# Four attention layers on one core: nine hand-written tables of steps put in another order

## The chip, the cores and the metric

The kernel runs on one core of one Trainium2 chip. The metric is the device time of one execution in microseconds (us); less is better. Three timed executions and one profiled execution of the kernel before are given.

## What is computed

64 batches of 64 tokens with 256 features (`x`) pass through four cross-attention layers against the same context (`ctx_2048`, 64 batches of 64 keys with 256 features). In layer 0 the "sequence" is the 256 features and the 64 tokens are the channels. The mask is all true in the inputs, but the kernel reads it. Cut to what matters:

```python
# layer 0: channels are the 64 tokens, attention runs over the 256 features
Mn = conv1x1(Wn, bn, inorm(x));  Mm = conv1x1(Wm, bm, inorm(ctx))
A  = softmax(einsum('bct,bcs->bts', Mn, Mm));  Ml = conv1x1(Wl, bl, ctx)
x  = conv1x1(Wo, bo, einsum('bcs,bts->bct', Ml, A)) + x
# layers 1 and 2: 16 heads of 16 features
a  = layer_norm(ctx) * ln_gamma + ln_beta
Q, K, V = heads(x @ Wq.T), heads(a @ Wk.T), heads(a @ Wv.T)
x  = x + tanh(gate) * (softmax(Q K^T / 4, mask) V) @ Wo.T
# layer 3: one head of 256 features, no norm
x  = x + alpha * (softmax((x w_q^T)(ctx w_k^T)^T / 16) (ctx w_v^T)) w_o^T
```

## The kernel before

**Groups and software pipeline.** The 64 batches are worked in eight groups of eight (512 tokens). A group first goes through a front part (its x and context are turned, normalised and projected, and layer 0 is computed) and then through layers 1, 2 and 3. The program runs these staggered: iteration g of the loop computes layers 1 to 3 of group g and, in between, the front part and layer 0 of group g+1. A start-up (prologue) loads and prepares all weights and does the front part of group 0, and a last iteration (tail) has no next group.

**Engines.** TensorE (PE) does every product and every transpose. Wide products are exact sums of three: each operand is split into a high and a low part, and `split_product` (lines 389 to 391) multiplies high by high, high by low and low by high. ScalarE (ACT) makes the high parts, the exponentials, and most copies out of PSUM. VectorE (DVE) makes the low parts, the row maxima and the subtractions of them, the normalisations by the sums, and the residuals. GpSimd (POOL) normalises the next group and builds its mask matrix. SyncE (SP) issues the DMAs.

**What sets the order.** No scheduler does. Nine strings list the steps of an engine, one after the other: `PE_ORDER`, `ACT_ORDER`, `DVE_ORDER` for an iteration, `..._FIRST` for the start-up and `..._TAIL` for the last iteration. Each engine runs its own list in that order and waits, at each step, on semaphores. The PE list also hands out the eight PSUM banks: the n-th fill of a table goes to bank n modulo 8 (`fills_of`, line 113), so a step of PE waits until the occupant eight fills before it has been read out (`wait_banks`). A moved step therefore changes which release its successors wait for.

**Names of the steps** (layer number behind the letter, then a part):
- `xT`, `cT`, `nT`: x, context and normalised context turned (lines 454 and 469 on PE); `Mn`, `Mm`, `V0`: projections of layer 0 (526, 481).
- `S`: scores (646 for layer 0, 659 for layers 1 and 2, 670 for layer 3) and on DVE the maxima and subtraction (1029; 1033 and 1037; 1042 and 1045). `X`: the exponential on ACT (855, 860, 863); `X3` on DVE: sums of layer 3 (1051, 1053). `T`: the weights turned (679, 703), copied out by ACT (874, 876, 878). `A`: weightings, that is the product with the values (726 for layer 0, 733 for layers 1 and 2), and on DVE the division by the sums (1064 to 1070 for layer 0, 1076 and 1078 else).
- `Q`, `K`, `V`, `O`: query, key, value and output projections (389 to 391); `AT`: the result of a layer turned; `XN`, `PV`: the last turn and the last product of layer 3 (679, 558), with DVE line 1021.
- `H.n` on ACT and `L.n` on DVE: high and low part of one half of the state (841, 968). `Q1.0` and `Q1.1` need `L.0` and `L.1`, `Q2.0` and `Q2.1` need `L.2` and `L.3`. There is one buffer for a half, so `H.1` comes after `Q1.0`.
- `ST`, `MV`: statistics of the next group (1087, 1095). `SC`: the mask column of the group (847).
- Start-up only: `Wq1` and so on: a weight turned (620), its high part on ACT and its low part on DVE (1140); `MT`, `MS`: mask turned and summed (572, 587); `GT`: a few vectors turned (577), copied out by DVE (1115); `WB`: DVE builds the block matrices of layer 0's weights (1218), which `W0T` turns (581) and `W0` multiplies (584, 585); `M3`, `VW3`: products of layer 3's weights (598, 604); `NB`: DVE's factor for the normalisation, `NM`: ACT's normalisation (925); `KB`, `TG`, `ON`, `CL`: sums for biases, gates, ones, and clearing of the two value buffers (1167, 1170).
- `VB1`, `VB2`: the light bias products, sixteen records of matmuls with one column each (612), whose results are the output biases of layers 1 and 2. `VB2` also waits for both value buffers to be cleared.

Two waits that the code places, and which the reader needs later:

```python
if step == ("P", "VB2", 0):
    pe.wait_ge(values_clear, 4)
...
act.wait_ge(freed[bk], released(bk, nth))   # state_high: H.1 behind DVE's A0.7
act.activation(state_hl[0][:], (state_in if n < 2 else state)[:, :, half], ACT.Copy).then_inc(state_hi, 1)
```

## Time and profile before

| | us |
|---|---|
| median of three timed executions | 594.43 |
| lowest and highest of them | 593.25, 596.83 |
| the profiled execution | 594.29 |
| its span in the trace | 592.5 |
| TensorE busy in the span | 560.8 |
| VectorE busy | 472.4 |
| ScalarE busy | 463.5 |
| GpSimd busy | 120.8 |

The span runs from the first to the last record of the core; the profiled execution's own time is 1.8 us more. The timeline lists an engine's instructions in order of time, merged where they are alike: start, duration of the merged stretch, engine, line, operation, output and inputs, count, and in brackets the idle time before it and what ended it. A count on PE is of records: an fp32 matmul leaves two. Durations of neighbours overlap, since matmuls and the short engines' instructions are pipelined; the difference between two starts is the time that a step really takes of its engine. The table of stretches gives, for each stretch, the busy time of each engine and the granted TensorE clock (1.00 is 2.4 GHz, 0.50 is 1.2 GHz).

### The profile page before, as it was taken

The page shows a single profiled execution, that of the slowest core. Times are in us where ns is not written, and L with a number is a line of the kernel's source. Part 1 is how long each engine was busy: PE and PEld are TensorE (multiplying, and loading weights), DVE is VectorE, ACT ScalarE, POOL GpSimd, SP SyncE. Part 2 cuts the span into 40 slices and gives each one's busy share as a digit, 9 for nine tenths or more (in the row PEclk, how much of TensorE's full clock was granted, in tenths as well). Part 3 has the DMA queues.
Part 4 walks back from the last instruction along what each step waited for, and adds up shares of the span by engine and source line. Part 5 has one row for each costly group of instructions (what it writes and reads, how often), then busy time and mean ns, then how long its engine had stood idle before and what let it go on. Part 6 is the DMA issues. An engine that isn't in the chain of part 4 may idle for free.

```text
span 592.5 us, 26503 instructions
## 1 busy us (share of the span) xinstructions
PE 560.8 (95%) x11087; PEld 495.9 (84%) x11087; DVE 472.4 (80%) x1063; ACT 463.5 (78%) x961; POOL 120.8 (20%) x138
## 2 busy tenths in 40 slices
...
DMA packets 18274, 18.36 MB, mean 31 GB/s; under 512 B 1553, under 2 KB 18065, under 8 KB 18177
## 3 DMA queue, kind: packets, MB, share of 16 engines
...
## 4 chain that ended last, share of the span: by engine, by line
PE 76%; ACT 11%; DVE 5%; issue 4%; DMA 2%; SPq 1%; DVEq 0%; ACTq 0%
PE psum L389 13%; PE psum L679 11%; PE psum L733 11%; PE psum L391 10%; PE psum L390 10%; ACT work L860 5%; PE psum L726 5%; PE psum L646 4%; PE psum L659 3%; ACT v L809 3%; DMA kbd<-in_L_xattn_Wq_dram 2%; PE psum L469 2%; PE psum L526 2%; PE psum L454 1%; PE psum L558 1%
## 5 line engine op out<-in xcount | busy, mean ns | idle before, releaser
L1033 DVE TENSOR_REDUCE negmax<-psum 128x8 f32<-128x512 f32 x128 | 87.3, 682 | 7.8 <-PE psum L659 7.7
L1037 DVE TENSOR_TENSOR shifted<-psum,negmax 128x512 f32<-128x512 f32 x128 | 88.5, 692 | 5.2
L874 ACT ACTIVATE work<-psum,group_mask 128x512 f32<-128x512 f32 x128 | 80.4, 700 | 7.4 <-PE psum L679 6.9
L860 ACT ACTIVATE work<-shifted 128x512 f32<-128x512 f32 x128 | 75.3, 632 | 3.1 <-DVE shifted L1037 1.9
L679 PE MATMUL psum<-const,work 64*128 64x64 f32 x1536 | 64.0, 226 | 10.5 <-ACT work L860 7.3
L679 PEld LDWEIGHTS psum<-const,work 64*128 64x128 f32 x1536 | 55.5, 139 | 21.9 <-ACT work L860 12.7
L733 PEld LDWEIGHTS psum<-v,work 128*64 128x64 f32 x2048 | 63.1, 138 | 8.4 <-issue 3.0
L733 PE MATMUL psum<-v,work 128*64 128x34 f32 x2048 | 67.7, 225 | 1.5 <-ACT work L874 1.4
L809 ACT ACTIVATE v<-psum 64x256 f32<-64x256 f32 x128 | 49.9, 390 | 19.0 <-PE psum L391 17.8
L855 ACT ACTIVATE work<-psum,negmax 128x256 f32<-128x256 f32 x128 | 50.8, 483 | 5.5 <-DVE negmax L1029 4.9
L1239 POOL TENSOR_SCALAR var_eps<-mean_var 128x8 f32<-128x8 f32 x8 | 2.0, 250 | 225.6 <-DVE mean_var L1095 225.5
L801 ACT ACTIVATE kbd<-psum,own_bias,const 128x512 f32<-128x512 f32 x64 | 46.7, 793 | 0.3 <-PE psum L391 0.3
L876 ACT ACTIVATE work<-psum 128x512 f32<-128x512 f32 x64 | 36.9, 617 | 8.3 <-PE psum L679 8.3
L1029 DVE TENSOR_REDUCE negmax<-psum 128x2 f32<-128x512 f32 x64 | 40.2, 681 | 0.7 <-PE psum L646 0.4
L659 PE MATMUL psum<-kbd,work 32*64 32x128 f32 x2048 | 38.7, 279 | 0.7 <-ACT work L820 0.7
L389 PE MATMUL psum<-wT_v_hi,nT_hi 128*128 128x256 f32 x128 | 39.1, 305 | 0.0
L389 PE MATMUL psum<-state_hi,wT_q_hi 128*128 128x256 f32 x128 | 37.9, 296 | 0.0
L389 PE MATMUL psum<-attnT_hi,wT_o_hi 128*128 128x256 f32 x128 | 36.9, 288 | 0.1
L1002 DVE TENSOR_TENSOR attnT_lo<-psum,attnT_hi 128x256 fp32r<-128x256 f32 x64 | 24.1, 418 | 15.9 <-ACT attnT_hi L825 15.7
L391 PE MATMUL psum<-wT_v_hi,nT_lo 128*128 128x256 f32 x128 | 36.5, 286 | 0.0
L390 PE MATMUL psum<-wT_v_lo,nT_hi 128*128 128x256 f32 x128 | 36.3, 283 | 0.0
L825 ACT ACTIVATE attnT_hi<-psum 128x256 fp32r<-128x256 f32 x64 | 21.2, 386 | 19.1 <-PE psum L679 18.9
...
## 6 DMA issues: line engine op xcount, KB each, us to landing
...
```

The lines of the kernel that those rows point to most:

```text
L389: pe.matmul(o, lh, rh, start=first, stop=False)
L390: pe.matmul(o, lh, rl, start=False, stop=False)
L391: return pe.matmul(o, ll, rh, start=False, stop=last)
L659: mm_ = pe.matmul(to[C * c:C * c + C, P * n:P * n + P], queries[rows, k, C * b:C * b + C], kbd[l - 1][rows, k, b].rearrange("p q s -> p (q ...
L679: mm_ = pe.transpose(banks[h][:, C * n:C * n + C], src[rows], ident[rows, rows])
L733: mm_ = pe.matmul(o[C * c:C * c + C, 2 * VW * j:2 * VW * (j + 1)], probsT[:, at + c, C * j:C * j + C], v2[l - 1][:, 2 * i + c, j].rearrang ...
L809: ins = act.activation(values[C * q:C * q + C, c, q, :, :, 0:HD], o[C * c:C * c + C, :].rearrange("k (p j q v) -> k q p j v", p=2, q=2, v= ...
L855: ins = act.activation(probs[:, exp_row(g, 0, i, last), D * u:D * u + D], psum[bk][:, D * u:D * u + D], ACT.Exp, bias=negmax0[:, i, u:u + 1])
L860: act.activation(probs[:, exp_row(g, l, i, last), :], shifted[:, i % 4, :], ACT.Exp).then_inc(exps, 1)
L874: act.activation(probsT[:, at, :], o[:], ACT.Copy, scale=group_mask[:, 2 * i + c:2 * i + c + 1]).then_inc(free, 1)
L1033: dve.tensor_reduce(negmax[:, i % 2, :], sv, AX_X, ALU.max, negate=True).then_inc(rowmax, 1)
L1037: dve.tensor_tensor(shifted[:, i % 4, :].rearrange("t (j k) -> t j k", k=C), sv, negmax[:, i % 2, :].unsqueeze(2).broadcast_to([P, NJ, C]) ...
```

## The change

Only the nine strings differ; no operation, size or wait is added or removed. The steps that are moved, and with them the PSUM banks:

- Start-up, PE: `cT` goes before `Wq1`, `Wq2` and `GT` before `Wk1`; `VB1` before `V0`; `A0.0-3` follow `S0.4-7` at once, with `Wk2`, `VW3`, `Wo2` and `K1.1` set between later steps; `VB2` goes from before `Q1.0` to behind it, the last step of the start-up.
- Start-up, DVE: `MT` before `ST.0`; `cT` and `Wq1` before the end of the statistics; `GT` before `WB`; both `CL` behind `S0.7`. ACT follows PE.
- Iteration, PE: `Q1.1` before `V2.0`; `V3.1` before `Q2.1`; `A0.0 S3.0 A0.1 S3.1` in place of `S3.0 A0.0-1 S3.1`; `T3.1` before `K1.1`.
- Iteration, DVE: `ST.0` goes from behind `S1.7` to the head of the iteration, before `S1.0`; at the end `L.0` goes from before `X3` to behind `A0.5`, and `X3.1` behind `A0.7`. ACT: `X1.0` before `Q1.1`, `X1.1` before `V2.0`, `K3.0` before `AT1.0`, `H.0` and `T3.0` before `T0.6`, `T3.1` behind `XN`.
- Tail: the same for `Q1.1`; on DVE `L.3` goes from behind `S2.0` to before it.

Two of the tables from the diff:

```diff
 PE_FIRST = """
-    xT.0-1 MT.0 MS.0 Wq1.0 Wk1.0 cT.0-1 Wq2.0 GT.0 W0T.0 W0.0 Wv1.0 nT.0-1 Wo3T.0 Mn.0-1 Mm.0-1 Wo1.0 Wo2.0 M3.0 K1.0
-    S0.0-3 V0.0-1 VB1.0 T0.0-3 S0.4-7 Wk2.0 VW3.0 A0.0-3 T0.4-7 K1.1 A0.4-7 Wv2.0 VB2.0 Q1.0
+    xT.0-1 MT.0 MS.0 cT.0-1 Wq1.0 Wq2.0 GT.0 Wk1.0 W0T.0 W0.0 Wv1.0 nT.0-1 Wo3T.0 Mn.0-1 Mm.0-1 Wo1.0 M3.0 K1.0 S0.0-3
+    VB1.0 V0.0-1 T0.0-3 S0.4-7 A0.0-3 T0.4-5 Wk2.0 K1.1 VW3.0 T0.6-7 Wo2.0 A0.4-7 Wv2.0 Q1.0 VB2.0
 """
 DVE_ORDER = """
-    S1.0-7 ST.0 A1.0-1 ST.1 AT1.0 ST.2-3 MV.0 O1.0 L.2 A1.2-3 AT1.1 O1.1 L.3 S2.0-3 V0.0-1 Mn.0-1 S2.4-7 Mm.0-1 A2.0-1
-    cT.0-1 nT.0-1 A2.2 S0.0-2 AT2.0 S0.3 A2.3 O2.0 AT2.1 S0.4-7 O2.1 S3.0 A0.1 S3.1 A0.3 L.0 X3.0-1 A0.5 A0.7 PV.0-1 L.1
+    ST.0 S1.0-7 ST.1 A1.0-1 ST.2 AT1.0 ST.3 MV.0 O1.0 L.2 A1.2-3 AT1.1 O1.1 L.3 S2.0-3 V0.0-1 Mn.0-1 S2.4-7 Mm.0-1 A2.0-1
+    cT.0-1 nT.0-1 A2.2 S0.0-2 AT2.0 S0.3 A2.3 O2.0 AT2.1 S0.4-7 O2.1 S3.0 A0.1 S3.1 A0.3 X3.0 A0.5 L.0 A0.7 X3.1 PV.0-1
+    L.1
```

The first place: PE, the start of the start-up, from the mask's transpose to the normalised context. `const,kbd` is a turned weight (x8: two of them), `const,c_raw` is `cT`, `const,scale_row` is `GT`, `const,scratch` is `W0T`, `mix,c_norm` is `nT`. Before:

```order
L572 MATMUL psum<-const,mask_f 128x32
L587 MATMUL psum<-mask_col,const 128x32
L620 MATMUL psum<-const,kbd 128x128 x8
L454 MATMUL psum<-const,c_raw 128x64 x16
L620 MATMUL psum<-const,kbd 128x128 x4
L577 MATMUL psum<-const,scale_row 128x10
L581 MATMUL psum<-const,scratch 128x128 x3
L584 MATMUL psum<-w0T,attn 128x128
L585 MATMUL psum<-w0T,scratch 128x128
L620 MATMUL psum<-const,kbd 128x128 x4
L469 MATMUL psum<-mix,c_norm 64x64 x32
```

and now:

```order
L572 MATMUL psum<-const,mask_f 128x32
L587 MATMUL psum<-mask_col,const 128x32
L454 MATMUL psum<-const,c_raw 128x64 x16
L620 MATMUL psum<-const,kbd 128x128 x8
L577 MATMUL psum<-const,scale_row 128x10
L620 MATMUL psum<-const,kbd 128x128 x4
L581 MATMUL psum<-const,scratch 128x128 x3
L584 MATMUL psum<-w0T,attn 128x128
L585 MATMUL psum<-w0T,scratch 128x128
L620 MATMUL psum<-const,kbd 128x128 x4
L469 MATMUL psum<-mix,c_norm 64x64 x32
```

The turns of the context have moved up before the first weight, and one weight (`Wk1`) has moved behind the third (`Wq2`) and `GT`.

The second place: PE, the end of the start-up. The row of `v,work` is `A0.4-7`, `const,kbd` is `Wv2`, `v_bias` is `VB2` (each of its two rows stands there twice), `state_hi,wT_q` is `Q1.0` (its three rows stand there four times), `wT_v,nT` is `V1.0` of the first iteration. Before:

```order
L726 MATMUL psum<-v,work 64x65 x32
L620 MATMUL psum<-const,kbd 128x128 x4
L612 MATMUL psum<-v_bias,wT_o_hi 128x1 x2
L612 MATMUL psum<-v_bias,wT_o_lo 128x1 x2
...
L389 MATMUL psum<-state_hi,wT_q_hi 128x256
L390 MATMUL psum<-state_lo,wT_q_hi 128x256
L391 MATMUL psum<-state_hi,wT_q_lo 128x256
...
L389 MATMUL psum<-wT_v_hi,nT_hi 128x256
```

and now:

```order
L726 MATMUL psum<-v,work 64x65 x32
L620 MATMUL psum<-const,kbd 128x128 x4
L389 MATMUL psum<-state_hi,wT_q_hi 128x256
L390 MATMUL psum<-state_lo,wT_q_hi 128x256
L391 MATMUL psum<-state_hi,wT_q_lo 128x256
...
L612 MATMUL psum<-v_bias,wT_o_hi 128x1 x2
L612 MATMUL psum<-v_bias,wT_o_lo 128x1 x2
...
L389 MATMUL psum<-wT_v_hi,nT_hi 128x256
```

The light products have moved behind the first queries.

The third place: DVE, the end of an iteration, as one piece of the difference. `state_lo` is `L.0`, `sums` and `recip<-sums` are an `X3`, the three rows from `recip<-psum` to `state_in` are `A0.5` and then `A0.7`:

```order
-L968 TENSOR_TENSOR state_lo<-state_in,state_hi 128x512
 L1051 TENSOR_REDUCE sums<-probs 128x2
 L1052 ISA
 L1053 RECIPROCAL recip<-sums 128x2
+L1064 RECIPROCAL recip<-psum 128x4
+L1067 TENSOR_TENSOR psum<-psum,recip 128x4x64
+L1070 TENSOR_TENSOR state_in<-psum,xT 128x2x2x64
+L967 ISA
+L968 TENSOR_TENSOR state_lo<-state_in,state_hi 128x512
```

The low part `L.0` has moved behind the division `A0.5`, which waits for PE.

## Rows read from the trace of the kernel before

**Rows 1.** The page, its first part: busy time of TensorE

```profile
PE 560.8 (95%) x11087; PEld 495.9 (84%) x11087; DVE 472.4 (80%) x1063; ACT 463.5 (78%) x961; POOL 120.8 (20%) x138
```

**Rows 2.** Waits of PE: line <- what it waited for: us, times, longest us

```profile
PE psum L679 <- ACT work L860: 7.3, 17, 0.8
...
PE psum L679 <- ACT work L855: 1.0, 2, 0.7
```

**Rows 3.** Timeline of PE, first 21 us: start, us, line, count [idle before]

```profile
9.74 0.63 PE L587 MATMUL psum<-mask_col,const 128*128 128x32 f32 x2 [1.84 <-DVE mask_col L1104]
...
12.06 1.12 PE L454 MATMUL psum<-const,c_raw 64*128 64x64 f32 x16
15.34 1.08 PE L620 MATMUL psum<-const,kbd 128*128 128x128 f32 x4 [2.16 <-DMA kbd<-in_L_xattn_Wq_dram]
...
18.11 0.80 PE L584 MATMUL psum<-w0T,attn 128*128 128x128 f32 x2 [0.65 <-DVE w0T L1117]
...
20.50 1.84 PE L469 MATMUL psum<-mix,c_norm 64*64 64x64 f32 x64 [0.31 <-DVE wT_k_lo L1140]
```

**Rows 4.** Timeline of DVE in the start-up

```profile
8.86 0.73 DVE L1087 BATCH_NORM_STATS2 stats<-x_raw 128x6 f32<-128x256 f32 x2
9.52 0.16 DVE L1104 COPY mask_col<-psum 128x32 f32<-128x32 f32 x1
...
14.23 1.41 DVE L1218 COPY scratch<-scratch 64x256 f32<-64x256 f32 x2
16.67 0.17 DVE L1115 COPY scale_col<-psum 128x10 f32<-128x10 f32 x1 [1.03 <-PE psum L577]
...
45.71 1.87 DVE L1167 MEMSET v<- 128x2176 f32 x1 [0.40 <-issue]
```

**Rows 5.** Timeline of PE: second light products, first repeat of values, `nT` in an iteration

```profile
48.09 0.61 PE L612 MATMUL psum<-v_bias,wT_o_hi 128*128 128x1 f32 x4 [0.96 <-DVE v L1170]
...
57.13 0.39 PE L389 MATMUL psum<-wT_v_hi,nT_hi 128*128 128x256 f32 x1
...
166.97 1.16 PE L469 MATMUL psum<-mix,c_norm 64*64 64x64 f32 x64
```

**Rows 6.** Stretches of 1 us: busy PE, PEld, DVE, ACT, POOL, then granted clock

```profile
49.00:50.00 1.00, 1.00 (x9) 1.00 (x8) 0.93 (x5) 0.00 (x0) 0.00 (x0) 0.67 0.00 0
50.00:51.00 1.00, 1.00 (x6) 1.00 (x7) 0.93 (x5) 0.00 (x0) 0.00 (x0) 0.50 0.00 0
...
56.00:57.00 1.00, 1.00 (x64) 0.96 (x64) 0.00 (x0) 0.98 (x3) 0.00 (x0) 0.91 0.08 16
```

**Rows 7.** Timeline of PE around the end of an iteration

```profile
254.87 0.27 PE L703 MATMUL psum<-const,probs 128*128 128x128 f32 x1
...
258.11 0.38 PE L389 MATMUL psum<-state_hi,wT_q_hi 128*128 128x256 f32 x1
...
268.34 0.88 PE L679 MATMUL psum<-const,work 64*128 64x64 f32 x19 [0.49 <-ACT work L860]
```

**Rows 8.** Timeline of DVE around the end of an iteration

```profile
255.73 0.27 DVE L1051 TENSOR_REDUCE sums<-probs 128x2 f32<-128x128 f32 x1
...
256.27 0.18 DVE L1064 RECIPROCAL recip<-psum 128x4 f32<-128x4 f32 x1
...
258.31 1.65 DVE L1021 SCALAR_TENSOR_TENSOR attn<-psum,recip,attn 128x256 f32<-128x256 f32 x4
260.92 0.69 DVE L968 TENSOR_TENSOR state_lo<-state_in,state_hi 128x512 fp32r<-128x512 f32 x1 [0.96 <-ACT state_hi L841]
262.23 0.69 DVE L1033 TENSOR_REDUCE negmax<-psum 128x8 f32<-128x512 f32 x1 [0.62 <-PE psum L659]
```

**Rows 9.** The tail: two rows of DVE's timeline, then one of PE's

```profile
561.32 0.69 DVE L1033 TENSOR_REDUCE negmax<-psum 128x8 f32<-128x512 f32 x1 [0.16 <-PE psum L659]
...
562.72 0.68 DVE L968 TENSOR_TENSOR state_lo<-state,state_hi 128x512 fp32r<-128x512 f32 x1
...
568.30 1.22 PE L679 MATMUL psum<-const,work 64*128 64x64 f32 x32 [0.60 <-ACT work L860]
```

More of the change, by code:

```diff
@@ L38 @@
 PE_ORDER = """
-    V1.0 S1.0-3 V2.0 Q1.1 V3.0 S1.4-7 T1.0-1 V1.1 A1.0-1 K3.0 T1.2 AT1.0 T1.3 K2.0 O1.0 A1.2-3 K2.1 AT1.1 Q2.0 O1.1 xT.0-1
-    S2.0-3 V2.1 Q2.1 V3.1 V0.0-1 Mn.0-1 T2.0 S2.4-7 T2.1 Mm.0-1 K3.1 A2.0-1 cT.0-1 T2.2 nT.0-1 T2.3 A2.2 S0.0-1 AT2.0
-    S0.2-3 A2.3 K1.0 O2.0 AT2.1 T0.0-1 S0.4-7 T0.2-3 O2.1 S3.0 A0.0-1 S3.1 A0.2-3 T0.4-7 XN.0-1 T3.0 K1.1 T3.1 A0.4-7
+    V1.0 S1.0-3 Q1.1 V2.0 V3.0 S1.4-7 T1.0-1 V1.1 A1.0-1 K3.0 T1.2 AT1.0 T1.3 K2.0 O1.0 A1.2-3 K2.1 AT1.1 Q2.0 O1.1 xT.0-1
+    S2.0-3 V2.1 V3.1 Q2.1 V0.0-1 Mn.0-1 T2.0 S2.4-7 T2.1 Mm.0-1 K3.1 A2.0-1 cT.0-1 T2.2 nT.0-1 T2.3 A2.2 S0.0-1 AT2.0
+    S0.2-3 A2.3 K1.0 O2.0 AT2.1 T0.0-1 S0.4-7 T0.2-3 O2.1 A0.0 S3.0 A0.1 S3.1 A0.2-3 T0.4-7 XN.0-1 T3.0-1 K1.1 A0.4-7
     PV.0-1 Q1.0
@@ L44 @@
 ACT_ORDER = """
-    V1.0 V2.0 Q1.1 X1.0-3 V3.0 SC.0 T1.0 X1.4 T1.1 X1.5-7 V1.1 AT1.0 K3.0 T1.2-3 H.2 K2.0 AT1.1 K2.1 Q2.0 H.3 xT.0-1 V2.1
-    X2.0-1 Q2.1 V3.1 X2.2-3 Mn.0-1 T2.0-1 Mm.0 X2.4-5 K3.1 Mm.1 X2.6-7 cT.0 T2.2 cT.1 nT.0-1 T2.3 AT2.0 X0.0-3 K1.0 AT2.1
-    T0.0-1 X0.4 T0.2 X0.5-6 T0.3 X3.0 X0.7 T0.4 X3.1 T0.5-6 H.0 T3.0 T0.7 T3.1 XN.0-1 K1.1 Q1.0 H.1
+    V1.0 X1.0 Q1.1 SC.0 X1.1 V2.0 X1.2-3 V3.0 T1.0 X1.4 T1.1 X1.5-7 V1.1 K3.0 AT1.0 T1.2-3 H.2 K2.0 AT1.1 K2.1 Q2.0 H.3
+    xT.0-1 V2.1 X2.0-1 V3.1 Q2.1 X2.2-3 Mn.0-1 T2.0-1 Mm.0 X2.4-5 K3.1 X2.6 Mm.1 X2.7 cT.0 T2.2 cT.1 nT.0-1 T2.3 AT2.0
@@ L48 @@
+    X0.0-3 K1.0 AT2.1 T0.0-1 X0.4 T0.2 X0.5-6 T0.3 X0.7 X3.0 T0.4 X3.1 T0.5 H.0 T3.0 T0.6-7 XN.0-1 T3.1 K1.1 Q1.0 H.1
 """
 DVE_ORDER = """
[L50 to L51 removed]
+    ST.0 S1.0-7 ST.1 A1.0-1 ST.2 AT1.0 ST.3 MV.0 O1.0 L.2 A1.2-3 AT1.1 O1.1 L.3 S2.0-3 V0.0-1 Mn.0-1 S2.4-7 Mm.0-1 A2.0-1
@@ L56 @@
 """
 ACT_FIRST = """
-    xT.0 Wq1.0 xT.1 cT.0-1 Wq2.0 Wk1.0 TG.0 NM.1 NM.0 Wv1.0 nT.0-1 Mn.0-1 Mm.0 Wo3T.0 Mm.1 Wo2.0 Wo1.0 M3.0 K1.0 X0.0-3
-    T0.0-3 Wk2.0 X0.4-7 VW3.0 T0.4-6 H.0 T0.7 Wv2.0 Q1.0 H.1 K1.1
+    xT.0-1 cT.0-1 Wq1.0 Wq2.0 Wk1.0 NM.1 NM.0 Wv1.0 nT.0 TG.0 nT.1 Mn.0-1 Mm.0-1 Wo1.0 Wo3T.0 M3.0 K1.0 X0.0-3 T0.0-3
+    X0.4-6 T0.4 H.0 X0.7 T0.5 Wk2.0 VW3.0 T0.6-7 K1.1 Wo2.0 Q1.0 Wv2.0 H.1
 """
 DVE_FIRST = """
-    ST.0 MT.0 ST.1 MS.0 ST.2-3 MV.0 WB.0 GT.0 TG.0 W0T.0 NB.0 Wq1.0 cT.0 Wk1.0 cT.1 Wq2.0 W0.0 KB.1 Wv1.0 ON.0 nT.0-1
```

12 lines of the change are left out of this document (6 added, 6 removed).

## The prediction, made before the result was known

> **What bounds the kernel now.** I read the page first: TensorE (PE) is busy 560.8 of 592.5 us [rows 1], so at most 31.7 us are idle, and a change of order can win only idle time or time at the lower clock. Then the waits of PE: the largest that repeats is L679, the turns of layers 1 and 2, behind ACT's exponential L860, 7.3 us in 17 waits [rows 2]. Then the timeline of PE, stage by stage. Up to 21 us it waits four times, 1.84, 2.16, 0.65 and 0.31 us [rows 3]. Later in the start-up it waits 1.0 us for layer 0's exponentials [rows 2] and 0.96 us before the second light products [rows 5]. From 58 us on it is nearly gapless; one of the two repeated waits for L860 is 0.49 us an iteration [rows 7], ended by the chain S1.3 on DVE, X1.3 on ACT. The table of stretches shows the last loss: the granted clock falls in the stretch from 49 us to 0.67, stays at 0.50 and comes back in the stretch from 56 us (0.91) [rows 6]. The sixteen light matmuls, one column each, lie just ahead of the fall, with the wait of 0.96 us.
>
> The times below are sums on the profiled execution, 594.29 us, which is 0.14 under the median of the runs shown, so I need no correction. The measurement tells about 1% (6 us) from no change.
>
> **Start-up, first 22 us.** DVE copies the mask column before the first statistics, so `MS` on PE starts some 0.66 us earlier than at 9.74 (the two rows' starts, 8.86 and 9.52 [rows 4]), at 9.1. `cT` follows (1.12) and one weight (half of a pair, about 1.0, by the 1.08 of a single one), so PE is done at 11.7 and waits for the fourth weight's load, which nothing moves: 15.34 [rows 3]. Idle is 3.6 there in place of 2.16, while `Wk1`, which used to fill it, now lies behind: with the second weight, `GT` and `Wk1` PE is at 17.6. On DVE `GT` waits until 16.67 as before and only then `WB` runs, 1.41 [rows 4], so `W0T` starts at 18.3. It takes 0.9, its copy another 0.6, and `W0` starts at 19.9 in place of 18.11: +1.8. `W0` and `Wv1` take what they took, 2.1, and `nT` starts at 22.0 in place of 20.50, its wait of 0.31 gone: **+1.5 us**. ACT's normalisation does not cover it: its factor NB ends at about 18.3, as late as before within 0.2, since POOL's chain in front of it is unchanged. Bounds: +0.8 (`WB` not behind `GT`'s wait) to +2.0.
>
> **Start-up, 22 to 57 us.** `A0.0-3` directly behind `S0.4-7`, and the turns `T0.4-5` and `T0.6-7` apart, give the exponentials room: the waits of 1.0 us [rows 2] go. The clearing of both value buffers is long done when `VB2` comes, so its 0.96 us goes too [rows 5]: **-1.9**. What is late next: both clearings now stand on DVE between `S0.7` and the low part of `Wk2`. One costs 0.40 + 1.87 + 0.5 = 2.8 us (its last row [rows 4], and the two small writes behind it, up to `VB2`'s release at 48.1). Two, 5.5 us behind some 41, end at 46.4; `Wk2`'s low part, whose bank `Wv2` on PE needs, ends at 47.2, and `L.0`, which `Q1.0` needs, at 47.9, where PE would come at 47.4 by my count of its steps. **+0.7**, with bounds 0 and 2.
>
> **The clock.** The stretch at the lower clock costs PE 0.33 in its first us, half of six us, and 0.09 in the last: 3.4 us of full-clock work [rows 6]. In the changed order `VB2` stands between `Q1.0` and `V1.0`, both dense, and follows no wait. The first light products, `VB1`, stand between dense steps now and no stretch there is below 1.00. I take it that the fall goes: **-3.4**, bounds -3.4 and 0. At the other end, PE starts at the low rate: `nT` takes 1.84 us at 20.5 us and 1.16 in an iteration [rows 3, 5], though the table of stretches does not show it as low there. If the rise follows the onset of steady work, it moves with `W0` by 1.8 us and costs 0.9; if not, nothing; if it comes half a low stretch later, 1.7. I take **+0.4**.
> The Trainium skill, "TensorE: Matmul & The Clock Gate", section "Part 4: PE-mode transpose", speaks against this reordering: transposes do not count as the engine being busy in the same way and do not bring the full clock. By that rule everything ahead of `W0` but the mask sum is idle for the clock, the rise waits for `W0`, and the term would be +0.9 in place of +0.4; the trace agrees so far as that the transposes of the start-up all run at the low rate.
>
> No moved step issues a DMA. SP holds the next group's loads until `V0` is filled, so they leave some 2 us later in the start-up; they are wanted first by `ST.0` at the head of the first iteration, 15 us behind: 0.
>
> **Start-up in sum:** 1.5 - 1.9 + 0.7 - 3.4 + 0.4 = -2.7. PE starts the step behind the first scores of layer 1 at about 54.4 in place of 57.13 [rows 5].
>
> **Iteration, seven times.** The wide products take as long in any order. `T3.1` behind `T3.0` saves a change of kind of matmul, at most its 0.27 us [rows 7]: I take -0.1. `A0.0 S3.0 A0.1` adds one: +0.05. `V3.1` before `Q2.1` gives `L.3` 1.4 us of room that it did not need: 0. `K3.0` before `AT1.0` on ACT falls in ACT's idle time: 0; on ACT `X1.3` still starts when DVE's S1.3 is ready, since `V2.0`, 1.6 us, fits between `X1.1` and `X1.2`: 0 with 0.05 of room.
> On DVE the end of the iteration gets tight. `A0.5` waits for PE and starts at 256.27; an `A0` step takes 1.02 (two from 256.27 to 258.31) [rows 8]. `L.0` now stands behind it and ends at 257.9, where `Q1.0` on PE starts at 258.11 [rows 7], 258.0 with `T3.1`'s gain: cover 0.1, price 0.05. Then `A0.7` 1.02, `X3.1` at most 0.54 (255.73 to 256.27), and the last sums 1.6: 261.0 in place of 259.9, and two of the banks of `S1.0-3`, which PE wants at 261.0, are released only there. `L.1` still starts at 260.9 to 261.0 behind `H.1` [rows 8], then `ST.0` with 0.66 fills DVE's idle 0.62 before `S1.0` at 262.23 [rows 8]. Nothing is left there for the branch of the loop. Bounds: 0, and the whole 0.66; I take +0.1, since the rows put the chain within 0.1 of PE. Behind a late `S1.0` stand S1.1 to S1.3, X1.3, and PE at the wait of 0.49. Sum of an iteration: -0.1 + 0.05 + 0.05 + 0.1 = +0.1, rounded: **+0.6 for seven**, bounds -1.2 and +5.
>
> **Tail.** On DVE `L.3` (0.6 by the starts) now stands before `S2.0`, but its input is ready only at about 561.85, so `S2.0` starts at 562.5 in place of 561.32 and S2.1 0.56 later than it did [rows 9]. From there DVE works without a pause up to S2.7, and PE waits for it through ACT (0.60 at 568.30 [rows 9]): **+0.6**, bounds 0 and 0.8.
>
> **Total:** 594.29 - 2.7 + 0.6 + 0.6 = 592.8 us.
>
> **Rivals.**
> 1. The clock falls all the same, with the light products merely later: 592.8 + 3.4 = 596.2. For it: they are the only light work near the fall. Against: `VB1` with the same sixteen records and no wait causes none. 17%.
> 2. Slower, by one mechanism: DVE at the head of the iteration. If `L.1`, the loop's branch and `ST.0` together come late by the whole 0.66 us, each S1 step, X1.3 and the turn on PE come late by it, seven times 4.6 in place of the 0.7 taken: 596.7. It decides from 0.3 us an iteration on (0.1 + 1.5/7). For it: no slack is left in the rows. Against: the idle 0.62 is just as long as the step. 13%.
> 3. The clock's rise in the start-up comes later by 1.7 us' worth: 594.1. 13%.
> 4. The start-up wins more than counted: `WB` runs early and the clearings hide (-0.7 and -0.7), and DVE's head costs nothing (-0.7): 590.7. 12%.
> 5. The forecast itself, 592.8: 45%.
>
> **How the numbers follow.** Two in ten is to be left out: the low end lies 1.3 under rival 4 plus half of what is open in the iterations, 589.3; the high end takes in rivals 1 and 2 alone but not together, 597.3. Faster by over 1% (under 588.5) needs gains that I do not see: 5%. Slower by over 1% (over 600.4) needs rivals 1 and 2 together or rival 2 beyond its price: 5%. The rest, 90%, is within 1%.
>
> **What would show it.** Right: no stretch at clock 0.50 near 50 us; PE idle of 3 to 4 us before 15.34; `W0` near 19.9; `VB2` without a wait; the wait of L679 for L860 unchanged at 0.49; in the tail S2.1 half a us later. Wrong: a fall of the clock behind `VB2`; DVE's S1.0 more than 0.2 us behind the end of PE's first S1 step; a wait of PE at L659 or at `Q1.0` in every iteration.

## The result, and the profile after

| us | before | changed |
|---|---|---|
| median | 594.37 (20 runs, 592.35 to 596.83) | 595.72 (20 runs, 593.97 to 597.74) |
| profiled execution | 594.29 | 596.31 |
| its span | 592.5 | 594.1 |

The ratio is 1.0029, with a 95% interval of 1.0017 to 1.0042. That is within 1%, as predicted, and inside the range, but on the wrong side: 1.35 us slower where I forecast 1.5 us faster. The question for the runs is what the iterations cost, and how much of the start-up's gain is there in every execution.

The first part of the page, which answers to [rows 1]: TensorE's busy time is as before, and the span is 1.6 us longer, so idle time has been added.

```profile
PE 560.5 (94%) x11087; PEld 494.3 (83%) x11087; DVE 471.0 (79%) x1063; ACT 464.8 (78%) x961; POOL 123.9 (21%) x138
```

The waits of PE, which answer to [rows 2]: line <- what it waited for: total us, times, longest. The waits for L855 (1.0) and before the light products are gone. Three new ones stand out: L659 behind DVE's L1021, seven times 0.4, L659 behind L1037, once in the tail, and L620 behind L1140, once in the start-up.

```profile
PE psum L679 <- ACT work L860: 6.8, 17, 0.8
...
PE psum L659 <- DVE attn L1021: 2.7, 7, 0.4
...
PE psum L659 <- DVE shifted L1037: 1.1, 1, 1.1
...
PE psum L620 <- DVE wT_k_lo L1140: 0.8, 1, 0.8
```

PE's timeline up to 25 us, which answers to [rows 3] (start, duration, in brackets the idle time before it). The wait for the fourth weight is 3.36, as forecast. The weight itself was there 0.44 earlier than in the profile before (14.90 for 15.34). `W0` starts at 19.06, not at the predicted 19.9. `nT` starts 0.57 later than before. Then the low clock lasts longer: 1.99 for `nT` and 1.64 for the first `Mn`, which took 1.84 and 1.09.

```profile
8.81 0.64 PE L587 MATMUL psum<-mask_col,const 128*128 128x32 f32 x2 [0.90 <-DVE mask_col L1104]
...
14.90 1.09 PE L620 MATMUL psum<-const,kbd 128*128 128x128 f32 x4 [3.36 <-DMA kbd<-in_L_xattn_Wq_dram]
...
19.06 0.79 PE L584 MATMUL psum<-w0T,attn 128*128 128x128 f32 x2 [0.83 <-DVE w0T L1117]
...
21.07 1.99 PE L469 MATMUL psum<-mix,c_norm 64*64 64x64 f32 x64
22.98 1.11 PE L592 MATMUL psum<-const,state 128*128 128x128 f32 x4
24.03 1.64 PE L526 MATMUL psum<-x_norm,w0T 64*64 64x256 f32 x16
```

DVE in the start-up, which answers to [rows 4]: `WB` takes 0.58 behind `GT`, where it took 1.41 before, and the two clearings stand in a row.

```profile
16.63 0.58 DVE L1218 COPY scratch<-scratch 64x256 f32<-64x256 f32 x2
...
41.72 1.87 DVE L1167 MEMSET v<- 128x2176 f32 x1 [0.40 <-issue]
...
44.56 1.87 DVE L1167 MEMSET v<- 128x2176 f32 x1 [0.52 <-issue]
```

PE at the end of the start-up, which answers to [rows 5]: `Wv2` waits 0.78 behind the clearings, the second light products wait for nothing, and the step behind the first scores starts at 54.48, where it was 57.13 and I forecast 54.4.

```profile
47.85 0.66 PE L620 MATMUL psum<-const,kbd 128*128 128x128 f32 x4 [0.78 <-DVE wT_k_lo L1140]
...
50.04 0.50 PE L612 MATMUL psum<-v_bias,wT_o_hi 128*128 128x1 f32 x4
...
54.48 0.38 PE L389 MATMUL psum<-state_hi,wT_q_hi 128*128 128x256 f32 x1
```

The table of stretches, which answers to [rows 6]: around the light products the granted clock stays at 1.00.

```profile
50.00:51.00 1.00, 1.00 (x12) 1.00 (x10) 0.93 (x4) 0.77 (x2) 0.00 (x0) 1.00 0.00 0
51.00:52.00 1.00, 1.00 (x10) 1.00 (x11) 0.96 (x3) 0.65 (x3) 0.00 (x0) 1.00 0.00 0
```

PE around the end of an iteration, which answers to [rows 7]. From the start of `PV.0` (L558) to `Q1.0` nothing is lost. `S1.0` (L659) then waits 0.39 and starts 4.49 behind `PV.0`, where before it was 4.01.

```profile
255.21 1.09 PE L558 MATMUL psum<-scratch 64*64 64x256 f32 x16
256.25 0.37 PE L389 MATMUL psum<-state_hi,wT_q_hi 128*128 128x256 f32 x1
...
259.70 1.20 PE L659 MATMUL psum<-kbd,work 32*64 32x128 f32 x64 [0.39 <-DVE attn L1021]
...
266.94 1.43 PE L679 MATMUL psum<-const,work 64*128 64x64 f32 x32 [0.49 <-ACT work L860]
268.29 0.39 PE L389 MATMUL psum<-wT_v_hi,nT_hi 128*128 128x256 f32 x1
```

DVE at the same place, which answers to [rows 8]. `A0.5` starts 0.81 ahead of `PV.0`, as before. `L.0` costs 0.60 (255.43 to 256.03) and `X3.1` 0.64 (257.04 to 257.68), and both now lie in front of the last sums, L1021. These end at 259.34, and PE goes on 0.36 later. `ST.0` behind them costs nothing, since DVE still waits 0.23 for PE.

```profile
254.40 0.18 DVE L1064 RECIPROCAL recip<-psum 128x4 f32<-128x4 f32 x1 [2.79 <-PE psum L726]
...
255.43 0.68 DVE L968 TENSOR_TENSOR state_lo<-state_in,state_hi 128x512 fp32r<-128x512 f32 x1
256.03 0.17 DVE L1064 RECIPROCAL recip<-psum 128x4 f32<-128x4 f32 x1
...
257.04 0.28 DVE L1051 TENSOR_REDUCE sums<-probs 128x2 f32<-128x128 f32 x1
...
257.68 1.66 DVE L1021 SCALAR_TENSOR_TENSOR attn<-psum,recip,attn 128x256 f32<-128x256 f32 x4 [0.16 <-DVE recip L1053]
...
259.85 0.75 DVE L1087 BATCH_NORM_STATS2 stats<-x_raw 128x6 f32<-128x256 f32 x2
260.83 0.69 DVE L1033 TENSOR_REDUCE negmax<-psum 128x8 f32<-128x512 f32 x1 [0.23 <-PE psum L659]
```

The tail, which answers to [rows 9]: on DVE `L.3` holds `S2.0` back, and then on PE the second block of scores of layer 2 waits 1.07, where it waited 0.69 for ACT.

```profile
563.68 0.68 DVE L1033 TENSOR_REDUCE negmax<-psum 128x8 f32<-128x512 f32 x1
```

```profile
568.10 1.20 PE L659 MATMUL psum<-kbd,work 32*64 32x128 f32 x64 [1.07 <-DVE shifted L1037]
```

**The account of the two profiled executions.** I measure from three starts on PE: the step behind the first scores, the `PV.0` of the last iteration, and the end of the span.

| stage | before | changed | difference |
|---|---|---|---|
| up to the step behind the first scores | 57.13 | 54.48 | -2.65 |
| from there to the seventh `PV.0` | 474.45 | 477.87 | +3.42 |
| from there to the end of the span | 60.92 | 61.75 | +0.83 |

The sum is +1.6, the difference of the spans. The start-up ended where it was forecast in this execution; the iterations gave it back. The middle stage holds six turns of the loop's end, each with a `S1.0` that comes 0.48 later, 2.9 us. Another 0.3 is idle time of PE for which the trace shows no cause ("issue"), one gap of 0.8 us before and two of 0.5 and 0.6 now. About 0.2 stays unplaced. The seventh late `S1.0` lies in the last stage.

### The profile page after: what moved, and what is told of

The parts are those of the page before. It is cut to its first block, busy times and chain, and to the rows that moved or that the text cites. A ratio compares the mean times of both kernels' runs of the same rounds, so it can differ in the third digit from the quotient of the medians.

```text
span 594.1 us, 26509 instructions
## 1 busy us (share of the span) xinstructions
PE 560.5 (94%) x11087; PEld 494.3 (83%) x11087; DVE 471.0 (79%) x1063; ACT 464.8 (78%) x961; POOL 123.9 (21%) x138
## 4 chain that ended last, share of the span: by engine, by line
PE 71%; ACT 11%; DVE 9%; issue 5%; POOL 2%; DVEq 0%; ACTq 0%; POOLq 0%
PE psum L389 11%; PE psum L679 11%; PE psum L733 11%; PE psum L391 9%; PE psum L390 9%; ACT work L860 5%; PE psum L726 4%; PE psum L646 4%; PE psum L659 3%; ACT v L809 3%; DVE shifted L1037 2%; PE psum L469 2%; DVE negmax L1033 2%; PE psum L526 2%; PE psum L454 2%
## 5 line engine op out<-in xcount | busy, mean ns | idle before, releaser
L1037 DVE TENSOR_TENSOR shifted<-psum,negmax 128x512 f32<-128x512 f32 x128 | 88.5, 692 | 5.3
L860 ACT ACTIVATE work<-shifted 128x512 f32<-128x512 f32 x128 | 76.6, 632 | 12.9 <-DVE shifted L1037 11.8
L855 ACT ACTIVATE work<-psum,negmax 128x256 f32<-128x256 f32 x128 | 51.3, 490 | 3.9 <-DVE negmax L1029 3.7
L659 PE MATMUL psum<-kbd,work 32*64 32x128 f32 x2048 | 38.8, 278 | 3.7 <-DVE attn L1021 2.7
L389 PE MATMUL psum<-wT_v_hi,nT_hi 128*128 128x256 f32 x128 | 37.8, 296 | 0.0
L1277 POOL TENSOR_SCALAR c_norm<-c_raw,mean_var,rstd 128x256 f32<-128x256 f32 x28 | 37.4, 1343 | 1.5 <-POOL rstd L1241 1.5
L659 PEld LDWEIGHTS psum<-kbd,work 32*64 32x64 f32 x2048 | 31.2, 130 | 7.6 <-issue 3.9
L1256 POOL TENSOR_SCALAR c_norm<-mrow_u 64x256 f32<-64x256 uint8 x16 | 6.4, 401 | 145.6 <-DMA mrow_u<-in_mask_dram 143.7
```

The source lines that it names most:

```text
L389: pe.matmul(o, lh, rh, start=first, stop=False)
L659: mm_ = pe.matmul(to[C * c:C * c + C, P * n:P * n + P], queries[rows, k, C * b:C * b + C], kbd[l - 1][rows, k, b].rearrange("p q s -> p (q ...
L855: ins = act.activation(probs[:, exp_row(g, 0, i, last), D * u:D * u + D], psum[bk][:, D * u:D * u + D], ACT.Exp, bias=negmax0[:, i, u:u + 1])
L860: act.activation(probs[:, exp_row(g, l, i, last), :], shifted[:, i % 4, :], ACT.Exp).then_inc(exps, 1)
L1037: dve.tensor_tensor(shifted[:, i % 4, :].rearrange("t (j k) -> t j k", k=C), sv, negmax[:, i % 2, :].unsqueeze(2).broadcast_to([P, NJ, C]) ...
```

## The experiments

Each ran in five rounds beside the kernel before, whose median was 593.69, 593.90 and 593.79 in the three sets of four. Tables written on fewer lines shift the line numbers by up to six: L659 is L657 or L653 in some rows. "Period" is the mean distance of neighbouring `PV.0` starts over the first three distances: (325.38 - 120.49) / 3 = 68.30 in the kernel before and (324.00 - 117.63) / 3 = 68.79 in the changed kernel. Later distances are longer in both, up to 69.19 and 69.82.

### First set: the parts, and DVE's end put back

**The start-up alone.**

```diff
-PE_FIRST, ACT_FIRST, DVE_FIRST: the tables of before
+PE_FIRST, ACT_FIRST, DVE_FIRST: the tables of the changed kernel
```

> The kernel before with the three start-up tables of the changed one, iterations and tail as before. Theory A (the start-up won what the two traces show, 2.7 us, of which 3.4 is the clock's fall that is gone, and the iterations gave back more): 591.5 to 592.5 in the timed runs, 2 to 3 us under before, no stretch below 1.00 near 50 us, the step behind the first scores of layer 1 at 54.5 in place of 57.1. Theory B (the fall of the clock comes and goes from run to run, the profile of before just had one): the start-up wins only some 0 to 1 us in the median, and the before runs beside it scatter by 3 us.

Measured: 591.87 us (12 runs), ratio 0.9975 [0.9959, 0.9990], which is 1.8 us faster. The period is 68.28, and from the last iteration's `PV.0` to the last one it takes 55.45, as before (55.42). But this profile has a fall of the clock again, in another place: it begins in the stretch from 32 us, behind the first light products, `VB1`.

```profile
31.00:32.00 1.00, 1.00 (x11) 1.00 (x10) 1.00 (x3) 1.00 (x4) 0.00 (x0) 1.00 0.00 0
32.00:33.00 1.00, 1.00 (x29) 0.98 (x31) 1.00 (x2) 1.00 (x4) 0.00 (x0) 0.89 0.03 8
33.00:34.00 1.00, 1.00 (x48) 1.00 (x46) 0.86 (x4) 0.80 (x3) 0.00 (x0) 0.50 0.00 0
```

**The iteration alone.**

```diff
-PE_ORDER, ACT_ORDER, DVE_ORDER: the tables of before
+PE_ORDER, ACT_ORDER, DVE_ORDER: the tables of the changed kernel
```

> The kernel before with the three iteration tables of the changed one, start-up and tail as before. Theory A: each of seven iterations is longer by 0.45 us for the first scores' wait for the banks of the last product, and by 0.1 at the second turn of layer 1, less 0.1 for the joined turns of layer 3: 3 to 3.5 us over before. Theory B: 1 us or less over before, the rest of what the traces show being scatter.

Measured: 597.44 us (6 runs), ratio 1.0073 [1.0056, 1.0091], 3.75 us slower; the period is 68.91. The wait of the changed kernel is there, seven times:

```profile
PE psum L660 <- DVE attn L1022: 2.6, 7, 0.4
```

This profile shows something else that bears on the clock. Its start-up is that of the kernel before, yet its clock falls twice: from 51 us (0.83), behind `VB2`, and from 34 us, right behind `VB1`, which starts at 32.51 there:

```profile
34.00:35.00 1.00, 1.00 (x19) 0.98 (x20) 0.51 (x2) 0.65 (x2) 0.00 (x0) 0.79 0.46 88
```

So the fall behind `VB1` is not a product of the new order.

**The tail alone.**

```diff
-PE_TAIL, ACT_TAIL, DVE_TAIL: the tables of before
+PE_TAIL, ACT_TAIL, DVE_TAIL: the tables of the changed kernel
```

> The kernel before with the three tables of the tail of the changed one. Theory A: 0.5 us over before, from the low part of the state that now stands ahead of the first maximum of layer 2 on DVE (the four turns behind them 0.55 us later, as the two traces show). Theory B: nothing that can be told from before.

Measured: 594.01 us (12 runs), ratio 1.0009 [0.9997, 1.0022], +0.3. The time from the last iteration's `PV.0` to the last one is 55.85 in place of 55.42, and the wait of L659 for L1037 (1.1) is there, so +0.43 in the trace, which the timing can't tell from nothing.

By the medians the three parts add up to -1.8 + 3.75 + 0.3 = +2.2, beside the +1.35 of all of them together; by the ratios it is -0.25% + 0.73% + 0.09% = +0.57% (3.4 us) beside +0.29% (1.7, interval 1.0 to 2.5 us). The signs and the order of size are plain, a sum to the microsecond is not.

**DVE's end of the iteration as before.**

```diff
-A0.3 X3.0 A0.5 L.0 A0.7 X3.1 PV.0-1 L.1
+A0.3 L.0 X3.0-1 A0.5 A0.7 PV.0-1 L.1
```

> The changed kernel with the end of DVE's iteration table put back (L.0 and both X3 before A0.5), nothing else. Theory A (DVE's last sums, 1.66 us behind L.0 and X3.1, release the two banks late): the wait of 0.39 us at L659 goes in all seven iterations, 2.7 to 3.2 us under the changed kernel, so about 592.8. Rival C (the cost is ST.0 at the head of DVE's iteration, or the order on ACT): the wait moves elsewhere and the time stays within 1 us of the changed kernel, 595 to 596.

Measured: 592.78 us (12 runs), ratio 0.9981 [0.9968, 0.9994]: 2.9 us under the changed kernel, by this one edit. `S1.0` starts 4.01 behind `PV.0` again and waits for nothing; the period is 68.40. `ST.0` still stands at the head of DVE's iteration here. The first maximum follows it without any idle time, 5.16 behind `PV.0`, where it came 5.15 behind (262.23 - 257.08) in the kernel before: with the scores on time, `ST.0` just fits.

```profile
254.88 1.09 PE L556 MATMUL psum<-scratch 64*64 64x256 f32 x16
...
258.89 1.21 PE L657 MATMUL psum<-kbd,work 32*64 32x128 f32 x64
```

```profile
260.04 0.69 DVE L1031 TENSOR_REDUCE negmax<-psum 128x8 f32<-128x512 f32 x1
```

### Second set: which step at DVE's end, and the light products elsewhere

**`X3.1` forward, `L.0` left where the change put it.**

```diff
-A0.3 X3.0 A0.5 L.0 A0.7 X3.1 PV.0-1 L.1
+A0.3 X3.0-1 A0.5 L.0 A0.7 PV.0-1 L.1
```

> The changed kernel with X3.1 alone put back before A0.5 on DVE; L.0 stays behind A0.5. Theory A1 (every instruction between A0.5 and the last sums counts, so X3.1's 0.64 us and L.0's 0.60 both delay the banks' release, and the wait of 0.39 is less than either): without X3.1 the last sums end 0.64 earlier, the wait at L659 goes wholly, about 3 us under the changed kernel, as with all of it put back. Rival A2 (L.0 behind A0.5 is what costs, through Q1.0 on PE): the wait stays or moves to Q1.0, within 1 us of the changed kernel.

Measured: 592.77 us (10 runs), ratio 0.9975 [0.9961, 0.9990]; period 68.38. With `L.0` alone in front of them the last sums start at 257.22, end at 258.87, and `S1.0` (L657) comes 4.02 behind `PV.0` without a wait. So the two steps are not costly each: together they pass the slack, and taking `X3.1` away takes the whole wait. Taking `L.0` away and leaving `X3.1` was not tried. The profile, the slowest of the ten runs, also has a fall of the clock far from any light product, in the stretches from 543 to 546 us, behind waits of 0.50 and 0.70.

```profile
255.40 1.09 PE L556 MATMUL psum<-scratch 64*64 64x256 f32 x16
...
259.42 1.21 PE L657 MATMUL psum<-kbd,work 32*64 32x128 f32 x64
```

```profile
257.22 1.65 DVE L1019 SCALAR_TENSOR_TENSOR attn<-psum,recip,attn 128x256 f32<-128x256 f32 x4
```

**`ST.0` back behind `S1.7`.**

```diff
-ST.0 S1.0-7 ST.1 A1.0-1 ST.2 AT1.0 ST.3 MV.0
+S1.0-7 ST.0 A1.0-1 ST.1 AT1.0 ST.2-3 MV.0
```

> The changed kernel with only the statistics on DVE put back behind the first eight maxima (ST.0 after S1.7). Theory A: ST.0 fills a pause of DVE that is there anyway, the first scores of layer 1 come late for another reason: within 0.5 us of the changed kernel, the wait of 0.39 at L659 unchanged. Rival C: ST.0 delays S1.0 and with it the turns of layer 1: 0.7 to 3 us under the changed kernel.

Measured: 595.91 us (12 runs), ratio 1.0033 [1.0018, 1.0049], no better than the changed kernel, with the period at 68.82 and the wait unchanged. The late scores could hide a cost of `ST.0` in this pair; the run with DVE's end put back, where they are on time, shows none beyond 0.01. My second rival, DVE's head of the iteration with `ST.0` in it, falls.

```profile
PE psum L657 <- DVE attn L1019: 2.6, 7, 0.4
```

**The start-up alone, with `VB1` between dense steps.**

```diff
-PE:  S0.0-3 VB1.0 V0.0-1 ... K1.1 VW3.0
+PE:  S0.0-3 V0.0-1 ... K1.1 VB1.0 VW3.0
-DVE: KB.2 VB1.0 V0.0-1 S0.4-6 A0.1 A0.3 S0.7 CL.0-1
+DVE: KB.2 V0.0-1 S0.4-6 A0.1 A0.3 S0.7 VB1.0 CL.0-1
```

> The kernel before with the start-up of the changed one, and VB1, the first light bias products, set between K1.1 and VW3, two dense steps, in place of between the scores and the values of layer 0. Theory D (the clock falls where light products lie beside other light steps): no run of it has a stretch at 0.50 near 33 or 50 us, every run's mean clock is 0.997 or more, and the median is 0.5 to 1.5 us under that of the start-up alone, with less scatter: 590.5 to 591.3. Rival E (the light products do it wherever they stand): the fall is there in as many runs, near 43 us, and the median is that of the start-up alone, 591.9 plus or minus 0.5.

Measured: 595.55 us (12 runs), ratio 1.0019 [1.0007, 1.0032], far from what I expected. I had put the read-out of `VB1` on DVE in front of the clearings, and there it waits 2.51 us for PE. The clearings and the low part of `Wk2` come that much later, and PE waits 2.67 us at `A0.6`. The clock then falls behind this wait (0.55 in the stretch from 52 us).

```profile
44.15 0.16 DVE L1110 COPY o_bias<-psum 128x2 f32<-128x2 f32 x1 [2.51 <-PE psum L609]
...
49.91 0.87 DVE L1137 SCALAR_TENSOR_TENSOR wT_k_lo<-psum,scale_col,wT_k_hi 128x256 fp32r<-128x256 f32 x2
```

```profile
50.94 1.15 PE L723 MATMUL psum<-v,work 128*64 128x65 f32 x32 [2.67 <-DVE wT_k_lo L1137]
```

**The same, and `T3.1` joined to `T3.0`.**

```diff
-PE:  XN.0-1 T3.0 K1.1 T3.1 A0.4-7
+PE:  XN.0-1 T3.0-1 K1.1 A0.4-7
```

> The kernel before it in this list (start-up of the changed kernel, VB1 between dense steps) with T3.1 directly behind T3.0 on PE, before K1.1, in each iteration. Theory A: a change of kind of matmul less, 0.1 us an iteration: 0.5 to 0.8 us under the kernel before it in this list, the period of an iteration 68.15 in place of 68.25. Rival: nothing, since T3.1's input or the copy behind it is late: the same period.

Measured: 595.30 us (12 runs), ratio 1.0023 [1.0007, 1.0038]. Its median is 0.25 under the run without the joining and its ratio higher, so the two are not told apart; the period is 68.26 beside 68.24. Its clock falls from 51 us (0.73), much as there.

### Third set: one step alone, and versions that might beat both

**`VB2` behind `Q1.0`, and nothing else.**

```diff
-PE_FIRST: ... A0.4-7 Wv2.0 VB2.0 Q1.0
+PE_FIRST: ... A0.4-7 Wv2.0 Q1.0 VB2.0
```

> The kernel before with one edit, the second light products behind Q1.0 instead of before it. If the place of these products behind their wait of 0.96 us makes the fall of the clock, both go: 0.96 + 3.4 us under the kernel before, ratio 0.9927. If a fall simply moves to the other light products, or behind this new place, in about half of the runs, as in the kernels with the new start-up: 0.96 and about half of 3.4 less, ratio 0.9955. If the fall stays in every run: only the wait goes, ratio 0.998. I expect the middle one; the granted clocks of the single runs (0.997 and more, or less) show which.

Measured: 591.32 us (12 runs), ratio 0.9975 [0.9958, 0.9991]. This one step gives the kernel before what the whole new start-up gives it, within what the measurement tells. Its profile has no stretch below 1.00 but the last (589 to 590), and the wait of 0.96 is gone. Not all of that reaches the end: PE is now early at the first scores and waits there 1.26 us for ACT, a wait that the slow clock had hidden. The step behind the first scores starts at 54.76 in place of 57.13, so in this order the wait and the fall together were worth 2.4 us and not 0.96 + 3.4.

```profile
48.89 0.50 PE L611 MATMUL psum<-v_bias,wT_o_hi 128*128 128x1 f32 x4
...
53.63 1.21 PE L658 MATMUL psum<-kbd,work 32*64 32x128 f32 x64 [1.26 <-ACT kbd L800]
54.76 0.39 PE L388 MATMUL psum<-wT_v_hi,nT_hi 128*128 128x256 f32 x1
```

In the twelve timed runs the mean granted clock was 0.998 or more in six (median 591.18) and lower in six (592.36). That is my middle case by the clocks, though the gain is nearer to the smallest of the three I had named.

**The changed kernel with DVE's end and ACT's head as before.**

```diff
-DVE: A0.3 X3.0 A0.5 L.0 A0.7 X3.1 PV.0-1 L.1
+DVE: A0.3 L.0 X3.0-1 A0.5 A0.7 PV.0-1 L.1
-ACT: V1.0 X1.0 Q1.1 SC.0 X1.1 V2.0 X1.2-3 V3.0 T1.0
+ACT: V1.0 V2.0 Q1.1 X1.0-3 V3.0 SC.0 T1.0
```

> The changed kernel with DVE's end of the iteration as before (as the run that was 592.78) and with ACT's head as before too (V1.0 V2.0 Q1.1 X1.0-3 V3.0 SC.0 T1.0). If the rest of the lengthening, 0.13 us at the pitch T1.0 to T1.1, comes from the order of ACT's copies, the period goes from 68.40 to 68.30 or below and the time is 0.7 to 0.9 us under that run: 591.9 to 592.1, ratio 0.9966. If it comes from PE's order (Q1.1 before V2.0), the period stays at 68.40 or gets longer, because PE then waits for V2.0's and Q1.1's banks in the other order: ratio 0.998 or above.

Measured: 602.92 us (6 runs), ratio 1.0146 [1.0118, 1.0174]: the slowest of all. ACT now copies `V2.0` before `Q1.1`, while PE still makes `Q1.1` first. ACT's copy waits 2.54 us, everything behind it on ACT waits too, and PE waits seven times for it.

```profile
266.83 1.59 ACT L805 ACTIVATE v<-psum 64x256 f32<-64x256 f32 x4 [2.54 <-PE psum L387]
268.45 0.60 ACT L816 ACTIVATE work<-psum 128x512 f32<-128x512 f32 x1
```

```profile
PE psum L655 <- ACT work L816: 6.2, 7, 0.9
```

So it answers another question than the one it was made for. The 0.13 us that I wanted to place (from `T1.0` to the next step on PE 1.35 in place of 1.22) stays open, and so does what is left in the period with DVE's end put back, 68.40 beside 68.30.

**The new start-up, and `T3.1` joined, nothing else in the iteration.**

```diff
-PE_ORDER: ... XN.0-1 T3.0 K1.1 T3.1 A0.4-7
+PE_ORDER: ... XN.0-1 T3.0-1 K1.1 A0.4-7
```

> The kernel before with the three new start-up tables, and T3.0-1 joined before K1.1 in the iteration. Beside the new start-up alone (591.87, ratio 0.9975) the joining saves one change of kind of matmul per iteration: 7 times 0.12 us = 0.8, so 591.0, ratio 0.9962. If the saving is lost at a later wait in the iteration (behind K1.1 or at T1.0), the period stays at 68.25 and the ratio at 0.9975.

Measured: 591.95 us (12 runs), ratio 0.9966 [0.9948, 0.9983]; period 68.28, the same as with the start-up alone. No saving can be seen. From the first `T3` (L700, L703) to `A0.4` (L723, L726) it takes 252.42 - 250.67 = 1.75 us joined and 252.55 - 250.78 = 1.77 apart, rows of this kernel and then of the start-up alone:

```profile
250.67 0.44 PE L700 MATMUL psum<-const,probs 128*128 128x128 f32 x2
...
252.42 2.09 PE L723 MATMUL psum<-v,work 128*64 128x65 f32 x64
```

```profile
250.78 0.33 PE L703 MATMUL psum<-const,probs 128*128 128x128 f32 x1
...
252.55 2.09 PE L726 MATMUL psum<-v,work 128*64 128x65 f32 x64
```

**That, with `VB1` dense, read out late, and the second clearing behind `L.0`.**

```diff
-PE:  S0.0-3 VB1.0 V0.0-1 ... K1.1 VW3.0
+PE:  S0.0-3 V0.0-1 ... K1.1 VB1.0 VW3.0
-DVE: S0.0-3 KB.2 VB1.0 V0.0-1 ... CL.0-1 Wk2.0 L.0 VW3.0
+DVE: S0.0-3 KB.2 V0.0-1 ... CL.0 Wk2.0 VB1.0 L.0 CL.1 VW3.0
```

> The kernel of e11_start_joined with the first light products between dense steps (behind K1.1), their read-out on DVE behind the low part of Wk2, and the second clearing behind L.0. DVE is held by nothing then: the wait of 0.78 us at Wv2 goes, and no new wait at A0.6 or at the first projection comes. If a fall of the clock needs light products or a long wait next to sparse steps, none is left: 0.8 + about 1.7 us under e11_start_joined, 588.6, ratio 0.992, all single runs at clock 0.998 or more. If the fall comes in half of the runs wherever the light products stand: only the 0.8, ratio 0.995.

Measured: 591.74 us (12 runs), ratio 0.9973 [0.9957, 0.9989], the same as the kernel it is built on (591.95), not the 588.6 I expected. The wait of 0.78 at `Wv2` is gone and `VB1` (L606 at 41.09) disturbs nothing. But `VB1` had covered layer 0's exponentials where it stood, and the turns `T0.0-3` now wait for them twice:

```profile
32.89 0.71 PE L673 MATMUL psum<-const,work 64*128 64x64 f32 x16 [0.56 <-ACT work L849]
34.35 0.71 PE L673 MATMUL psum<-const,work 64*128 64x64 f32 x16 [0.75 <-ACT work L849]
```

Its profile has no stretch below 1.00 up to 586 us, and the clock of its single runs was 0.998 or more in seven of twelve, 0.997 in four and 0.993 in one. So the place of the light products is not the only thing that brings a fall.

Of the versions tried, `VB2` alone behind `Q1.0` (591.32) has the lowest median and is the smallest edit. The start-up alone, with the joining and with the last edit lie within 0.7 us of it, and the intervals of the ratios overlap.

## Why the prediction was right or wrong, point by point

**The iteration: the term that failed.** I wrote "two of the banks of `S1.0-3`, which PE wants at 261.0, are released only there" and priced the release at 261.0 as just in time, so +0.1 us an iteration in all. This is the step that failed: the price of the late release. It cost 0.48 at this place and 0.5 an iteration in all, 3.4 us in seven and 3.75 in the run of the iteration alone, for a forecast of +0.6. The last of my own signs of being wrong, a wait at L659 in every iteration, came true. Three things made it up, reckoned from the start of `PV.0` at 257.08 in the trace of before. `L.0` and `X3.1` cost 0.60 and 0.64, not 0.54 for the latter, so the sums end at 257.08 + 4.13 = 261.21. PE goes on 0.36 behind that end, which I took as 0: 261.57. And PE wants the bank at 261.09. The difference is the 0.48. It recurs seven times and in the runs of the iteration alone and with `ST.0` back. The run with DVE's end put back took 2.9 us off the changed kernel; moving `X3.1` alone did it as well. The mechanism was thus in the text, without a rival of its own and at a price of nothing; the upper bound of +5 covers its size, but was reckoned from DVE's head.

Why is there so little room at this place? The opening says that a fill waits for the occupant eight fills before. That holds inside a table. The iteration's table has 108 fills, which is not a multiple of eight, and each iteration starts again at bank 0. So `PV.0` and `PV.1` lie in banks 1 and 2, and `S1.0` and `S1.1` of the next iteration want just these, only four fills later (`PV.1`, `Q1.0`, `V1.0`, `S1.0`). PE fills `S1.0-3` as one step and waits for all four of their banks. Whether another start of the count would remove the wait was not tried.

**The gain of the joined turns.** I took -0.1; it is 0.02 by the two rows above, and nothing by the period. I had read the duration of one small row (0.27) as time saved, where rows overlap and only the starts count.

**`ST.0` at the head of the iteration.** Right that DVE's idle time covers it. The 0.23 to spare in the changed kernel is there because the scores come late; with DVE's end put back it fits with nothing to spare, at a cost of 0.01. The second rival, 4.6 us by this step, had the right sign and nearly the right size (3.75 with the iteration's tables alone) and the wrong mechanism: the run with `ST.0` put back changed nothing.

**Start-up, first 22 us.** Forecast +1.5, measured +0.57 at `nT`. The wait for the weight (3.6 forecast, 3.36 measured) held. What was off is `WB` behind `GT`: I took the 1.41 of [rows 4], but behind `GT` it took 0.58. `W0T` then started at 17.36, not 18.3, and `W0` at 19.06, not 19.9, although `W0T`'s read-out had to wait on DVE behind the low part of `Wq2` (0.83 idle on PE).

**Start-up, 22 to 57 us.** The two waits went, -1.9, and the clearings came back with 0.78 where I took +0.7. Right. The step behind the first scores is at 54.48 by a forecast of 54.4, which is partly luck: the second L526 row, behind the clock's rise, starts at 25.50 in place of 23.77, so `nT`'s +0.57 and a late rise of 1.16 stand where I had +1.5 and +0.4, two misses that cancel. The next two points say more.

**The clock's fall.** Forecast: gone, -3.4. In the profiled execution it is gone. Over many executions it is not. The lists of runs give the mean clock of each, not where it fell. The three sets hold 91 timed runs of the kernel before; the mean granted clock is 0.998 or more in two of them, 591.84 and 592.19 us, the fastest two of their set. Of 84 runs of the seven kernels with the new start-up tables unaltered, 38 are at 0.998 or more, from 1 of 10 (`X3.1` forward) to 12 of 20 (the changed kernel). With the start-up alone the runs at 0.998 or more have a median of 590.53 and the others 593.33. So by the mean clock the new order runs free, or nearly, in something like half of its runs. Runs so marked are faster by 1.8 us in the kernel before (593.79 less the mean of the two) and by 2.8 in the start-up alone (the two medians), not by 3.4; in the other kernels with four or more runs of each kind it is 0.4 to 2.1. I had multiplied one execution's fall by a chance of one. That can account for the start-up alone giving 1.8 and not 2.7 us. It is an inference from means: they also hold falls at other places (from 543 us above, and near the end of the span), and the profile with `VB1` read out late has 0.998 with low stretches from 586 us on.

**The clock's rise.** Forecast +0.4. The Trainium skill, "TensorE: Matmul & The Clock Gate", section "Part 4: PE-mode transpose", would have made it +0.9. Seven profiled executions share the same start-up code, and they differ among themselves by more than either:

| kernel | `nT` | `Wo3T` | first `Mn` | first stretch below 1.00 |
|---|---|---|---|---|
| the changed kernel | 1.99 | 1.11 | 1.64 | none |
| start-up and joined turns | 1.99 | 1.12 | 1.58 | from 588 us (0.70) |
| `ST.0` back | 1.99 | 1.12 | 1.19 | from 34 us (0.77) |
| `X3.1` forward | 1.99 | 1.12 | 1.18 | from 34 us (0.76) |
| ACT's head as before | 1.99 | 0.91 | 1.09 | from 61 us (0.58) |
| start-up alone | 1.75 | 0.66 | 1.09 | from 32 us (0.89) |
| DVE's end back | 1.68 | 0.66 | 1.09 | from 32 us (0.86) |

The rise comes during `nT` in the last two and only in `Mn` in the first two, which costs some 1.1 us (the first layer-0 scores start at 30.18 in the changed kernel and at 29.04 in the start-up alone). So neither +0.4 nor +0.9 can be told from the scatter. The same page, section "Part 1: The HAM clock gate", says that the moment of the change is not tied to the kernel's start and differs between runs; these rows agree that it differs, and show nothing of what it is tied to.

**The tail.** Forecast +0.6 by `L.3` before `S2.0`. Measured +0.43 in the run of the tail alone, and by the mechanism named. The rest of the +0.83 in the changed kernel is the wait at the banks of `PV`, which the tail's first scores meet as well.

**The first rival** (the clock falls all the same, 596.2) is the other half of the result: by the mean clocks some fall is there in about half of the runs, though behind `VB1` in four of the seven profiles and nowhere behind `VB2`. My argument against it, that `VB1` causes none, rested on one profile of the kernel before; with the same start-up the run of the iteration alone has one there. The start-up's term, too large, and the iteration's, too small, make the sum: forecast -2.7 + 0.6 + 0.6, measured apart -1.8 + 3.75 + 0.3.
